# First attention computed transposed, and a second graph's softmax with one wide exponential

## The chip, the cores and the metric

The kernel runs on one core of one Trainium2 chip. The metric is the device time of one execution in microseconds (us). The engines are TensorE (PE, matmuls and transposes into PSUM), VectorE (DVE), ScalarE (ACT), GpSimd (POOL) and SyncE (SP, which issues the DMAs). Each works through its own queue of instructions in order; they wait for each other by semaphores.

## The reference

64 graphs of 128 nodes with 256 features go through four layers, each with a residual and a layer norm. The change touches the first and the last.

```
# layer 0, one graph
query = x @ Wq.T + bq ; keyt = x @ Wk.T + bk ; value = x @ Wv.T + bv
weight = adj * exp(query @ keyt.T)                  # [q, k], no maximum is taken
weight = weight / sum(weight, axis=k)
x = layernorm(x + weight @ value)
# layer 1: three graph convolutions, adj @ (x @ W) + b   (the kernel's gcn_...)
# layer 2: hypergraph convolution up to 512, layer norm, down to 256   (hyper_..., gram)
# layer 3, 8 heads of 32
scores = (q @ k.T) * scale * (2 * adj)              # [head, q, k]
attn = softmax(scores, axis=k)
x = layernorm(x + (attn @ v) @ Wo.T + bo)
```

## The kernel before

Four graphs make a group (`GB = 4`), so there are 16 groups (`NG`). Work on a group has three stages: A is layers 0 and 1, B is layer 2, C is layer 3. In one iteration the kernel does stage A of group t, stage B of group t-1 and stage C of group t-2, interleaved. The order on each engine is written out by hand as a table of step names: `PROLOGUE` (up to t = 2), `SCHEDULE` (12 iterations, t = 3 to 14, the loop is unrolled) and `EPILOGUE`. `run` walks the table; each name is a function for that engine, and the semaphore waits stand in the functions. So the table decides what is queued behind a wait. Weights are split into two fp32r parts (`high_...` by ACT, `rest_...` by DVE) in the prologue, and products are taken as high*high + rest*high + high*rest.

First attention in stage A. `att_t` and `att_t_rest` form t = att^T x, where att is the product of the two weight matrices made once in `set_att`. `att_scores` forms the scores of the four graphs with queries on the partitions. ACT adds a per-row offset in the exponential (`att_exp`, line 867), DVE multiplies by `adjA` (line 1120), PE transposes the four tiles (`att_turn`, line 579), ACT copies them back to SBUF (line 871), and only then `att_out` can multiply them with the values. The column of ones in `v0` makes the row sum, and DVE divides and adds the residual (lines 1125 and 1129). Two adjacency tiles are loaded per group in stage A: `adjA` for the mask and `adjTA`, the transposed one, for the graph convolutions and for `incidence`. The next `adjTA` is loaded only when the last convolution of the group is done.

Last attention in stage C. `mha_scores0` and `mha_scores1` on PE give the scores of graphs 0, 1 and of 2, 3. DVE multiplies each graph's 1024 columns by the mask (line 1245, the DVE step has the same name) and takes the maximum of each of 8 heads (`mha_max`, line 1250). For graphs 0, 1 and 2 ACT then runs 8 exponentials of 128 columns, each with its own bias and its accumulated sum (line 948). For graphs in `WHOLE`, before only graph 3, DVE subtracts the maximum over all 1024 columns (`mha_shift3`, line 1254), ACT runs one exponential of 1024 columns (line 953), and DVE sums (`mha_sum3`, line 1259). DVE takes the reciprocal (`mha_div`), POOL multiplies (line 1377), PE transposes (`mha_turn`, line 788).

Other waits that matter here. `gram` on PE waits for all four residuals of the first attention (`res0_ready`). `hyper_x` of stage B on PE waits until all four masked scores of stage C have left PSUM. `hyper_up01_rest` on PE waits for both halves of `gx_rest`, which DVE makes in `hyper_rest0` and `hyper_rest1` (line 1062). `gcn_1` waits for `gm_ready` from DVE's `gram_scale`. `keep_busy` is four dummy matmuls with `fill`, put where PE would otherwise wait.

## Time and profile before

| | us |
|---|---|
| median of 3 runs | 1061.04 (1059.98 to 1061.5) |
| profiled execution | 1061.14 |
| its span, first to last instruction | 1059.4 |
| PE busy | 1026.7 (97%) |
| DVE busy | 839.8 (79%) |
| ACT busy | 654.5 (62%) |
| POOL busy | 485.2 (46%) |

The busy time of an engine is the union of its instructions' times. A matmul's recorded time is longer than the step from one matmul to the next, because matmuls overlap; so steps between starts are the better measure on PE. In the 12 iterations of the loop the same pattern repeats every 61.4 us.

### The profile page before, as it was taken

To read this page: it belongs to the slowest core of one execution; us is meant where nothing else is said; L and a number is where in the kernel's file an instruction comes from. 1 tells how busy PE (TensorE), PEld (TensorE's weight loads), DVE (VectorE), ACT (ScalarE), POOL (GpSimd) and SP (SyncE) were. 2 spreads that over 40 slices of the span, in tenths; PEclk is the share of its full clock that TensorE was granted. 3 is DMA by queue.
4 is the path that set the end of the run, shared out by engine and by line. 5 is a ranking of instruction groups with operands and counts; after the bars stand their busy time and mean duration, and the time that the engine had idled before them with its cause. 6 is when DMAs were issued, how large, how long until landed. Compare 5 with 4: busy or idle time off the path is not lost.

```text
span 1059.4 us, 21720 instructions
## 1 busy us (share of the span) xinstructions
PE 1026.7 (97%) x8376; PEld 913.4 (86%) x8376; DVE 839.8 (79%) x2247; ACT 654.5 (62%) x1755; POOL 485.2 (46%) x298
## 2 busy tenths in 40 slices
PE   8899999999999999999999999999999999998876
PEld 7688898898989889898988889898988989897764
DVE  4666878878797888879788887978888797978566
ACT  3444855839475683948568394856839485673724
POOL 2315363745435364543536464353546445351613
PEclk9999999999999999999999999999999999999998
DMA  6110101011110101111010111101011110000001
GB/s 228 50 61 9 62 2 61 21 41 51 33 59 21 51 21 41 51 41 50 22 50 22 40 51 41 51 21 50 31 32 51 41 51 21 32 2 11 21 1 40
DMA packets 17383, 43.35 MB, mean 41 GB/s; under 512 B 2048, under 2 KB 2048, under 8 KB 17152
## 3 DMA queue, kind: packets, MB, share of 16 engines
q1 hardware_dynamic: 17280, 41.97, 11.8%
q8 instruction: 66, 1.08, 0.4%
q14 instruction: 37, 0.30, 0.1%
HBM read 33.57 MB, written 8.39 MB: 40 GB/s over the span
## 4 chain that ended last, share of the span: by engine, by line
PE 92%; ACT 3%; DVE 3%; issue 1%; POOL 0%; DMA 0%; POOLq 0%; SPq 0%; DVEq 0%
PE ps L476 83%; PE ps L788 5%; PE ps L729 1%; ACT pr L948 1%; PE ps L579 1%; PE ps L715 1%; DVE pr L1245 1%; PE ps L659 1%; DMA pr<-in_weights 0%; DVE mx L1250 0%; DVE st L1067 0%; DVE aT_rest L1147 0%; ACT aT_high L885 0%; POOL rstd L1331 0%; ACT up_high L925 0%
## 5 line engine op out<-in xcount | busy, mean ns | idle before, releaser
L948 ACT ACTIVATE pr<-pr,mx 128x128 f32<-128x128 f32 x384 | 149.4, 407 | 9.6 <-DVE mx L1250 9.6
L1377 POOL TENSOR_TENSOR pr<-pr,den 128x1024 f32<-128x1024 f32 x64 | 122.1, 1916 | 56.6 <-DVE den L1265 56.6
L1331 POOL TENSOR_TENSOR rstd<-var,neg_half 128x4 f32<-128x4 f32 (+1 forms) x84 | 73.5, 876 | 143.9 <-DVE var L1078 143.9
L1083 DVE TENSOR_SCALAR x<-x,mv,rstd 128x256 f32<-128x256 f32 x256 | 90.6, 417 | 38.8 <-POOL rstd L1331 38.0
L1356 POOL TENSOR_TENSOR x<-x,rows 128x1024 f32<-128x1024 f32 x16 | 38.1, 2381 | 178.6 <-PE ps L476 178.6
L1067 DVE BATCH_NORM_STATS2 st<-x 128x6 f32<-128x256 f32 x256 | 91.6, 415 | 0.7
L1361 POOL TENSOR_TENSOR up_rest<-upT,up_high 128x1024 fp32r<-128x1024 f32 x32 | 81.9, 2561 | 0.0
L1245 DVE TENSOR_TENSOR pr<-ps,adjB 128x1024 f32<-128x1024 f32 x64 | 75.2, 1218 | 7.3 <-PE ps L476 7.3
L948 ACT ACTIVATION_READ_ACCUMULATOR pr<-pr,mx 128x1 f32 x384 | 79.1, 206 | 0.0
L902 ACT COPY s_s<-ps 128x512 f32<-128x512 f32 x32 | 18.8, 587 | 95.2 <-PE ps L476 95.2
L1250 DVE TENSOR_REDUCE mx<-pr 128x8 f32<-128x1024 f32 x64 | 76.4, 1201 | 0.0
L942 ACT ACTIVATE qkT<-ps,biases 128x512 f32<-128x512 f32 x64 | 42.2, 688 | 55.1 <-PE ps L476 54.9
L476 PE MATMUL ps<-W_high,aT_high 128*128 128x256 f32 x256 | 69.9, 298 | 1.9 <-ACT aT_high L885 1.9
L788 PE MATMUL ps<-ident,pr 128*128 128x128 f32 x512 | 67.6, 275 | 3.8 <-POOL pr L1377 1.9
L1366 POOL TENSOR_TENSOR hv<-hv,neg_half 128x2 f32<-128x2 f32 x32 | 22.4, 701 | 103.6 <-DVE hv L1211 103.6
L476 PE MATMUL ps<-W_rest,aT_high 128*128 128x256 f32 x256 | 65.6, 281 | 0.0
L788 PEld LDWEIGHTS ps<-ident,pr 128*128 128x128 f32 x512 | 57.5, 142 | 8.7 <-issue 5.7
L476 PE MATMUL ps<-WdownT_high,up_high 128*128 128x258 f32 x256 | 64.3, 283 | 0.0
L476 PE MATMUL ps<-WdownT_rest,up_high 128*128 128x258 f32 x256 | 63.9, 282 | 0.0
L1269 DVE COPY pr<-ps 128x512 f32<-128x512 f32 x64 | 43.5, 679 | 17.3 <-PE ps L788 17.0
L1350 POOL TENSOR_TENSOR x<-x,rows 128x1024 f32<-128x1024 f32 x16 | 38.6, 2413 | 38.7 <-PE ps L476 38.7
L1147 DVE TENSOR_TENSOR aT_rest<-ps,aT_high 128x512 fp32r<-128x512 f32 x64 | 41.7, 676 | 17.7 <-ACT ps L898 10.9
(199 smaller groups left out, 3310.7 us busy)
## 6 DMA issues: line engine op xcount, KB each, us to landing
xT<-in_xT SPq DMA_DIRECT2D x16, 512.0 KB, 3.7
x<-in_x SPq DMA_DIRECT2D x16, 512.0 KB, 3.3
out_x<-x SPq DMA_DIRECT2D x32, 256.0 KB, 2.1
adjA<-in_adj SPq DMA_DIRECT2D x16, 256.0 KB, 2.7
adjTA<-in_adjT SPq DMA_DIRECT2D x16, 256.0 KB, 2.7
adjB<-in_adj SPq DMA_DIRECT2D x16, 256.0 KB, 2.9
pr<-in_weights SPq DMA_DIRECT2D x2, 512.0 KB, 6.0
qkT<-in_weights SPq DMA_DIRECT2D x1, 1024.0 KB, 12.1
```

What stands on the lines that cost most here:

```text
L476: return pe.matmul(out, lhsT, rhs, start=(k == 0), stop=(k == n - 1))
L788: last = pe.transpose(ps4[:, turn_bank(b) + k // 4, k % 4], pr[:, b, k, :], ident[:])
L942: act.activation(qkT[:, m, :], ps[:, 4 + m, :], ACT.Identity, bias=b_qk[:, m, :], scale=ATT if m < C else 1.0).then_inc(qk_ready, 1)
L948: act.activation(pr[:, b, k, :], pr[:, b, k, :], ACT.Exp, bias=mx[:, b, k:k + 1], accum_out=den[:, b, 0, k:k + 1]).then_inc(exp_ready, 1)
L1067: dve.bn_stats(st[i][:, b, :], t[:, b, :]).then_inc(norm_step[i], 1)
L1083: dve.tensor_scalar(t[:, b, :], t[:, b, :], mv[i][:, b, 0:1], rstd[i][:, b:b + 1], ALU.subtract, ALU.mult).then_inc(ready, 1)
L1245: dve.tensor_tensor(pr[:, b].rearrange("p (j i) n -> p j i n", i=C), ps4[:, 4:8, 2 * bb:2 * bb + 2, :], mask, ALU.mult).then_inc(masked_re ...
L1250: dve.tensor_reduce(mx[:, b, :], pr[:, b], AX.X, ALU.max, negate=True).then_inc(mx_ready, 1)
L1269: dve.tensor_copy(pr[:, b, 4:8, :], ps4[:, turn_bank(b) + 1]).then_inc(prT_dve, 1)
L1331: pool.tensor_tensor(rstd[i][:, bs], var[i][:, bs], neg_half[:, bs], ALU.pow).then_inc(rstd_ready[i], len(pairs))
L1361: pool.tensor_tensor(up_rest[:, fs, :], upT[:, fs, :], up_high[:, fs, :], ALU.subtract).then_inc(up_rest_ready, 1)
L1377: pool.tensor_tensor(pr[:, b], pr[:, b], den[:, b, 1, :].unsqueeze(2).broadcast_to([P, HEADS, P]), ALU.mult).then_inc(pr_ready, 1)
```

## The change

Scores of the first attention are formed transposed, with keys on the partitions. att is now built from the two weight matrices in the other order, and the vectors that carried the biases change places with it (`t0` and the extra column of `Wv0T`). The masked exponential is then already the operand that `att_out` needs: `att_turn` is gone from PE and ACT, and so are the tile `adjA` and its DMA. The mask is now the transposed adjacency, which has two tiles (`adjT[0]`, `adjT[1]`), loaded two groups ahead. `e0` and `p0T` are separate tiles. `WHOLE` becomes (1, 3). `set_att` is split into `set_att` and `set_vec`. All three order tables are new.

```
-WHOLE = (3,)
+WHOLE = (1, 3)
-        adjA = sb("adjA", [P, GB, P]); adjTA = sb("adjTA", [P, GB, P])
+        adjT = [sb(f"adjT{i}", [P, GB, P]) for i in range(2)]
-        e0 = p0 = sb("e0_p0", [P, GB, P])
-        p0T = sb("p0T", [P, N4]); rs0 = sb("rs0", [P, GB]); x0 = sb("x0", [P, GB, D])
+        e0 = sb("e0", [P, GB, P]); p0T = sb("p0T", [P, GB, P]); rs0 = sb("rs0", [P, GB]); x0 = sb("x0", [P, GB, D])
         def att_bank(b):
-            return (b + 2) % 4
+            return (2, 3, 1, 0)[b]
-            def next_adjTA(g):
-                if not final(g):
+            def later_adjT(g):
+                if g + 2 < NG:
                     sp.wait_ge(gcn_done, 2 * g + 2)
                     sp.wait_ge(inc_ready, g + 1)
-                    sp.dma_start(adjTA[:], A["adjT"][g + 1]).then_inc(adjTA_in, 16)
+                    sp.dma_start(adjT[g % 2][:], A["adjT"][g + 2]).then_inc(adjT_in[g % 2], 16)
...
-                        mm(ps[:, m, 0:D], wq0[:, o, m * P:(m + 1) * P], wk0[:, o, :], o, C)
+                        last = mm(ps[:, m, 0:D], wk0[:, o, m * P:(m + 1) * P], wq0[:, o, :], o, C)
+                    last.then_inc(att_mm, 1)
...
-            def att_turn(g):
-                if first(g):
-                    pe.wait_ge(ident_ready, 2)
+            def att_out(g):
                 for b in range(GB):
-                    pe.wait_ge(p0_ready, GB * g + b + 1)
-                    last = pe.transpose(ps4[:, 1, b], p0[:, b, :], ident[:])
-                last.then_inc(p0T_done, 1)
-
-            def att_out(g):
-                pe.wait_ge(p0T_ready, g + 1)
-                for b in range(GB):
+                    pe.wait_ge(p0T_ready, GB * g + b + 1)
...
-            def att_turn(g):
-                act.wait_ge(p0T_done, g + 1)
-                act.copy(p0T[:], ps[:, 1, :]).then_inc(p0T_ready, 1)
...
-                        dve.wait_ge(adjA_in, 16 * g + 16)
-                    dve.tensor_tensor(p0[:, b, :], e0[:, b, :], adjA[:, b, :], ALU.mult).then_inc(p0_ready, 1)
+                        dve.wait_ge(adjT_in[g % 2], 16 * (g // 2) + 16)
+                    dve.tensor_tensor(p0T[:, b, :], e0[:, b, :], adjT[g % 2][:, b, :], ALU.mult).then_inc(p0T_ready, 1)
 SCHEDULE, DVE:
-        ("C", "mha_max0"), ("A", "att_exp"), ("C", "mha_scores1"), ("C", "mha_max1"), ("C", "mha_div0"),
+        ("C", "mha_max0"), ("C", "mha_max1"), ("C", "mha_scores1"), ("C", "mha_max2"), ("C", "mha_shift1"),
```

The order that the tables give shows best in three places. The first is DVE in one iteration of the loop, from `incidence` and the masking of the last attention's scores (`pr<-ps,adjB`, two graphs a row) to `degrees`. `mx` are the maxima, `e_p` or `p0T` the masked exponentials of the first attention, `rs` and `x` its `att_out`, `fT_rest` are `hyper_rest0` and `hyper_rest1`. Before:

```order
411 L1177 TENSOR_TENSOR bhT<-hT,cnt 128x4x128
412 L1245 TENSOR_TENSOR pr<-ps,adjB 128x1024 x2
413 L1250 TENSOR_REDUCE mx<-pr 128x8
414 L1120 TENSOR_TENSOR e_p<-e_p,adjA 128x128 x4
415 L1245 TENSOR_TENSOR pr<-ps,adjB 128x1024 x2
416 L1250 TENSOR_REDUCE mx<-pr 128x8
417 L1265 RECIPROCAL den<-den 128x8
418 L1250 TENSOR_REDUCE mx<-pr 128x8
419 L1125 RECIPROCAL rs<-ps 128x1
```

And now:

```order
417 L1074 TENSOR_SCALAR x<-x,mv,rstd 128x256 x4
418 L1236 TENSOR_TENSOR pr<-ps,adjB 128x1024 x2
419 L1241 TENSOR_REDUCE mx<-pr 128x8 x2
420 L1236 TENSOR_TENSOR pr<-ps,adjB 128x1024 x2
421 L1241 TENSOR_REDUCE mx<-pr 128x8
422 L1245 TENSOR_TENSOR pr<-pr,mx 128x1024
423 L1111 TENSOR_TENSOR p0T<-e,adjT 128x128 x4
424 L1256 RECIPROCAL den<-den 128x8
425 L1053 TENSOR_TENSOR fT_rest<-ps,fT_high 128x512
426 L1116 RECIPROCAL rs<-ps 128x1
```

The mask of the first attention moved behind the second masking and behind the new subtraction (row 422).

The second place is DVE right behind that, up to the layer norm's statistics. Before:

```order
423 L1062 TENSOR_TENSOR fT_rest<-ps,fT_high 128x512
424 L1125 RECIPROCAL rs<-ps 128x1
425 L1129 SCALAR_TENSOR_TENSOR x<-ps,rs,x 128x256
426 L1125 RECIPROCAL rs<-ps 128x1
427 L1129 SCALAR_TENSOR_TENSOR x<-ps,rs,x 128x256
428 L1265 RECIPROCAL den<-den 128x8
429 L1062 TENSOR_TENSOR fT_rest<-ps,fT_high 128x512
430 L1067 BN_STATS st<-x 128x6 x4
```

And now:

```order
431 L1120 SCALAR_TENSOR_TENSOR x<-ps,rs,x 128x256
432 L1116 RECIPROCAL rs<-ps 128x1
433 L1120 SCALAR_TENSOR_TENSOR x<-ps,rs,x 128x256
434 L1250 TENSOR_REDUCE den<-pr 128x8
435 L1053 TENSOR_TENSOR fT_rest<-ps,fT_high 128x512
436 L1256 RECIPROCAL den<-den 128x8
437 L1058 BN_STATS st<-x 128x6 x4
```

A sum over 1024 columns (row 434) now stands in front of the second `fT_rest`.

The third place is ACT at the start of the kernel. `..._high` are the weight splits (`att_high` is the one that `att_t` needs), `xT_high` the split of the input. Before:

```order
1 L978 ACT_TABLE_LOAD
2 L978 CAST WoT_high<-upT 128x512
3 L978 CAST Wv3T_high<-upT 128x512
4 L978 CAST W_high<-pr 128x512
5 L978 CAST att_high<-upT 128x512
6 L978 CAST Wv0T_high<-pr 128x516
7 L906 CAST xT_high<-xT 128x1024
```

And now:

```order
1 L893 ACT_TABLE_LOAD
2 L893 CAST xT_high<-xT 128x1024
3 L965 CAST att_high<-upT 128x512
4 L965 CAST Wv0T_high<-pr 128x516
5 L965 CAST W_high<-upT 128x512
```

The splits of the input and of att now stand ahead of all others.

## Rows read from the trace of the kernel before

**Rows 1.** The page's first part: busy time of each engine.
```profile
PE 1026.7 (97%) x8376; PEld 913.4 (86%) x8376; DVE 839.8 (79%) x2247; ACT 654.5 (62%) x1755; POOL 485.2 (46%) x298
```
**Rows 2.** Busy time by stage: us, each engine's busy (instructions), clock, DMA share, GB/s.
```profile
0.00:25.00 25.00, 21.77 (x79) 18.06 (x80) 10.11 (x43) 8.71 (x13) 5.54 (x9) 1.00 0.64 242
320.00:950.00 630.00, 629.45 (x5326) 567.16 (x5324) 523.26 (x1389) 414.05 (x1107) 312.00 (x185) 1.00 0.11 37
```
**Rows 3.** The same view, one iteration cut at two places on PE.
```profile
481.07:496.56 15.49, 15.49 (x161) 14.20 (x161) 14.58 (x31) 12.46 (x55) 4.43 (x3) 1.00 0.19 52
496.56:542.50 45.94, 45.90 (x362) 41.14 (x361) 36.63 (x109) 27.97 (x55) 25.87 (x16) 1.00 0.11 36
```
**Rows 4.** Timeline of PE there: start, us, what, count.
```profile
481.07 1.17 PE L476 MATMUL ps<-qkT 32*128 32x128 f32 x32
...
489.66 0.60 PE L579 MATMUL ps<-ident,e_p 128*128 128x128 f32 x4
490.10 1.95 PE L476 MATMUL ps<-gmT,x 128*128 128x128 f32 x16
...
495.64 1.16 PE L476 MATMUL ps<-bhT,hT 128*128 128x129 f32 x8
496.56 1.18 PE L476 MATMUL ps<-fT_rest,WupT_high 128*128 128x512 f32 x4
```
**Rows 5.** Waits in two iterations: total us, times, longest.
```profile
PEld ps L476 <- DVE x L1129: 0.9, 2, 0.4
...
PEld ps L788 <- issue: 0.5, 2, 0.2
```
**Rows 6.** Timeline of DVE in the same iteration.
```profile
482.99 2.35 DVE L1245 TENSOR_TENSOR pr<-ps,adjB 128x1024 f32<-128x1024 f32 x2
485.25 1.21 DVE L1250 TENSOR_REDUCE mx<-pr 128x8 f32<-128x1024 f32 x1
486.38 0.89 DVE L1120 TENSOR_TENSOR e_p<-e_p,adjA 128x128 f32<-128x128 f32 x4
487.18 2.35 DVE L1245 TENSOR_TENSOR pr<-ps,adjB 128x1024 f32<-128x1024 f32 x2
...
492.52 0.17 DVE L1125 RECIPROCAL rs<-ps 128x1 f32<-128x1 f32 x1 [0.67 <-PE ps L476]
...
493.72 0.68 DVE L1062 TENSOR_TENSOR fT_rest<-ps,fT_high 128x512 fp32r<-128x512 f32 x1
494.31 0.16 DVE L1125 RECIPROCAL rs<-ps 128x1 f32<-128x1 f32 x1
...
501.24 1.19 DVE L1254 TENSOR_TENSOR pr<-pr,mx 128x1024 f32<-128x1024 f32 x1
```
**Rows 7.** The page: exponentials of the last attention, one head each.
```profile
L948 ACT ACTIVATE pr<-pr,mx 128x128 f32<-128x128 f32 x384 | 149.4, 407 | 9.6 <-DVE mx L1250 9.6
```
**Rows 8.** Timeline of ACT in the same iteration: one exponential over 1024 columns.
```profile
505.28 1.07 ACT L953 ACTIVATE pr<-pr 128x1024 f32<-128x1024 f32 x1
```
**Rows 9.** Timeline of ACT at the start of the kernel.
```profile
14.66 0.62 ACT L978 CAST WoT_high<-upT 128x512 fp32r<-128x512 f32 x1 [12.64 <-DMA upT<-in_weights]
```
**Rows 10.** Timeline of PE at the start of the kernel.
```profile
13.01 3.76 PE L476 MATMUL ps<-fill 128*128 128x512 f32 x8
...
20.80 0.58 PE L476 MATMUL ps<-xT_high,att_high 128*128 128x512 f32 x1
...
30.02 1.00 PE L579 MATMUL ps<-ident,e_p 128*128 128x128 f32 x4
31.69 2.01 PE L476 MATMUL ps<-v,p0T 128*128 128x257 f32 x8 [0.68 <-ACT p0T L871]
```
**Rows 11.** Timeline of DVE at the start of the kernel.
```profile
28.44 1.23 DVE L1056 TENSOR_TENSOR WdownT_rest<-pr,WdownT_high 128x1032 fp32r<-128x1032 f32 x1
```
**Rows 12.** Timeline of PE near the end of the kernel.
```profile
974.34 1.09 PE L476 MATMUL ps<-fill 128*128 128x512 f32 x4
...
992.21 1.06 PE L788 MATMUL ps<-ident,pr 128*128 128x128 f32 x8 [0.95 <-ACT upT L928]
```

More of the change, by code:

```diff
@@ new lines @@
+    "DVE": [("set_rep", 0), ("set_att", 0), ("rest_att", 0), ("set_vec", 0), ("rest_Wv0T", 0), ("set_reps", 0),
+        ("incidence", 0), ("rest_Wv3T", 0), ("rest_W2", 0), ("rest_WupT", 0), ("set_down", 0), ("att_exp", 0),
[22 rows of a table added]
+        ("high_WupT", 0), ("high_Wv3T", 0), ("att_v1", 0), ("att_off", 0), ("att_t", 0), ("att_exp", 0),
[18 rows of a table added]
+    "SP": [("att_scores", 0), ("att_out", 0), ("gcn_3a1", 0), ("att_scores", 1), ("att_out", 1), ("att_scores", 2),
+        ("gcn_3a1", 1), ("mha_scores1", 0), ("att_out", 2), ("x3_norm1", 0), ("x3_norm0", 0)],
@@ L645, in gcn_3a @@
                 for b in (2 * pair, 2 * pair + 1):
-                    last = mm(ps2[:, 2 + pair, b % 2], adjTA[:, b, :], s3[:, b, :])
+                    last = mm(ps2[:, 2 + pair, b % 2], adjT[g % 2][:, b, :], s3[:, b, :])
                 last.then_inc(gcn_done, 1)
```

97 lines of the change are left out of this document (46 added, 51 removed), and 302 rows, old and new, of tables (EPILOGUE, PROLOGUE, SCHEDULE).

## The prediction

> **What bounds the kernel now.** I read the page's busy times first: PE is busy 97% of the span, DVE 79%, ACT 62% [rows 1]. Then the busy time by stage: from 320 to 950 us PE is busy 629.45 of 630 us at the full clock, while in the first 25 us it is busy 21.77, part of that with dummy matmuls [rows 2]. So the loop is bound by PE, and a change is worth there what it does to PE's row of instructions; the ends of the kernel are bound by chains between engines. Third the timelines of one iteration [rows 4, 6]. One iteration lasts 61.43 us and I cut it where the last attention's scores start on PE (`mha_scores0`, 481.07) and where `hyper_up01_rest` starts (496.56): 15.49 and 45.94 us [rows 3]. In the first piece DVE is itself busy 14.58 of 15.49 us, in the second 36.63 of 45.94 [rows 3]. The reader is to see that the first piece is the one place of the loop where a second engine has hardly any room, and that the change puts DVE work just there. Fourth the waits: in the loop PE hardly waits, twice a short time per iteration [rows 5].
>
> **What it takes away on PE.** `att_turn` is 4 transposes; from their start to the next instruction 0.44 us pass (489.66 to 490.10) [rows 4]. That is 0.44 us per iteration at full value as long as PE bounds. The ACT copy behind it, the load of `adjA` and one SP queue entry go too; neither ACT (12.46 of 15.49 us in the piece) nor DMA (share 0.19) sets anything in the loop [rows 3], so I count them at nothing, and the cover that hides them is PE's own work. The second `adjT` tile frees the mask from waiting for a load; no row shows a wait for `adjTA` or `adjA` in the loop, so it is nothing too, below and above.
>
> **The wide exponential for graph 1.** ACT loses 8 exponentials of 128 columns, each 0.407 us long by the page [rows 7], and gets one of 1.07 us [rows 8]: 8 x 0.407 - 1.07, some 2 us of ACT per iteration, off the path in the loop. DVE gets a subtraction of 1.19 us and a sum over 1024 columns, which is the same kind of instruction with the same shape as the maximum, 1.21 us; the step from the maximum to the next instruction is 1.13 (485.25 to 486.38), so I count 1.1 for each of the two [rows 6]. So DVE carries 2.2 us more, and both stand in the tight piece.
>
> A rule of the Trainium skill speaks against this half: VectorE: DVE Perf Modes, section Rules for kernel authors, calls `tensor_reduce` the slowest DVE operation and advises to restructure where it is on a hot path. The rows show it no slower than the subtraction of the same width, 1.21 us for the maximum against 1.19 [rows 6]; by the rule the sum would cost more than the term below takes, by the rows it costs the same. It is the place, not the kind, that costs here.
>
> **The tight piece step by step.** DVE cannot start masking before the scores end on PE, 1.17 us into the piece [rows 4], about 0.05 later. Before, it came late (482.99), because `x1_norm` waited for POOL and `incidence` stood behind it [rows 6]; in the new order `incidence` stands ahead of `x1_norm`, fills that wait, and DVE is there in time. Then it has, up to the end of `hyper_rest1`, without a gap: two maskings of two graphs at 2.26 (482.99 to 485.25), three maxima at 1.13, the subtraction 1.1, the four masks of the first attention 0.80 (486.38 to 487.18), a reciprocal 0.1, `hyper_rest0` 0.59 (493.72 to 494.31), four rows of `att_out` at 1.20 a pair (492.52 to 493.72), the sum 1.1, and `hyper_rest1` to its end 0.68 [rows 6]. That is 4.52 + 3.39 + 1.1 + 0.80 + 0.1 + 0.59 + 2.40 + 1.1 + 0.68 = 14.68. With 1.17 in front and 0.05 at either end the piece lasts 15.95 us. PE alone needs 15.49 less 0.44 for the transposes and less about 0.15 for its wait before `gram`, which DVE's line 1129 ends (0.4 on the weight load, most of it under the matmul in front) [rows 5]: 14.9. So I expect PE to wait about 1.05 us there, 0.2 of it before `att_out` (the masks now stand behind the subtraction and come about when PE arrives) and 0.85 before `hyper_up01_rest`, because the sum stands in front of `hyper_rest1`. Behind that wait on PE are `hyper_up2`, `hyper_up3` and all the rest, in order, and everyone waits for PE. The piece grows by 15.95 - 15.49 = 0.46 us although PE has less to do.
>
> In the other piece `mha_turn1` no longer follows `mha_turn0` at once, which takes away a stall of 0.2 [rows 5]; DVE's `gram_scale` comes about when `gcn_1` wants it, which I put at 0.1 of wait. Net -0.1. Per iteration +0.36, for 12 iterations +4.3 us. Bounds: if no new wait showed, -0.44 - 0.15 - 0.2 = -0.8 an iteration, -9.6 in all; if both new DVE instructions (2.3 us) fell wholly on PE, less 0.8, +1.5 an iteration, +18. I take the value of the count, nearer to the lower row since PE has 14.9 us of cover.
>
> **The start.** Before, ACT's first instruction is a weight split that waits 12.64 us for its DMA, and the splits for `att_t` stand behind it; PE runs dummies for 3.76 us from 13.01 on and then `set_down`, before `att_t` starts at 20.80 [rows 9, 10]. Now `xT_high` and `att_high` come first, the dummies run while the first DMA is awaited, and `set_down` comes behind `att_v1`, when its weights have landed. So about 3.6 us of dummies leave the path (3.76 less the overlap with the next matmul). The first `att_turn` and its copy leave it too: 30.02 to 31.69, 1.67 us [rows 10]. Against that DVE's `rest_WdownT` (1.23 us, 1.15 as a step) now stands between the two halves of `att_out` [rows 11]. -3.6 - 1.67 + 1.15 = -4.1. Bounds: 0, if the DMA of `WupT`, whose split now stands ahead of `att_t` on ACT, holds it as long; -7, if all that stands between the first matmuls and 20.80 but `set_down` were gained as well.
>
> **The end.** The dummies before `mha_scores1` of group 14 go (974.34, 1.09 us recorded, some 0.9 as a step), and `mha_turn1` waits 0.95 us less for ACT, whose exponentials are shorter [rows 12]; in the last group the third POOL product comes some 0.6 earlier by the 2 us less on ACT against the DVE work put in. -2.5, with bounds -5 and +2, since DVE's two wide instructions lie on the chain of the last group, and a dummy in another place can let PE's clock fall, which the trace shows only at the very end.
>
> **The sum.** The profiled execution took 1061.14 us (span 1059.4), the median is 1061.04. 1061.04 + 4.3 - 4.1 - 2.5 = 1058.7 us. A measurement of this kernel tells about 0.2% (2.1 us) from no change.
>
> **Rivals.** (1) PE stays the only bound in the loop: DVE's row is shorter than I add it up, or PE's is longer, so that the new waits vanish. -0.8 x 12 - 4.1 - 2.5 gives 1044.8. For it: PE is busy 99.9% now [rows 2], and the order of before had only some 0.15 us of waits in the same piece. Against it: the step lengths are from rows of the same instructions, and they add up to more than PE's. This is also what Perfetto Trace Analysis of the Trainium skill, section Identifying the Most-Contended Engine, would make of it: relieve the engine with the highest occupancy first; by it the transposes count in full.
> (2) DVE's delay runs on. `max3`, `degrees`, `x0_norm` and `shift3` follow the sum, and `gram_scale` stands behind all of them; PE's `gcn_1` waits for it. I have PE arrive 0.1 before it. From that point each further 0.1 us on DVE costs 0.1 on PE; with 0.3 us on the first piece and 0.3 at `gcn_1` it is 0.6 more an iteration, +7.2: 1066. For it: DVE and POOL work side by side there, and DVE has no gap from the scores on. Against it: DVE is busy only 36.63 of the 45.94 us [rows 3].
> (3) The start and end gain nothing, since later waits take it back, and only the loop counts: 1065.3. Against it: the first 25 us are not full of needed work: 21.77 us busy with the dummies counted in [rows 2, 10].
>
> **Chances.** My count 0.47, its own range 1054.5 to 1062; rival 1 0.26; rival 2 0.17; rival 3 0.10. Faster by over 0.2% (below 1058.9): all of rival 1 and a bit over half of the count, 0.52. Within 0.2% (to 1063.2): 0.20, from the count. Slower: rivals 2 and 3, 0.28 with a rest of the count. The range 1046 to 1067 leaves 0.1 on each side: below it half of rival 1, above it the tail of rival 2.
>
> **What would show it.** In the changed kernel's trace: one iteration of 61.8 us; from the first `qkT` matmul to the first `fT_rest` matmul 15.9 us; PE waiting for `fT_rest` of DVE some 0.8 us in each iteration, and for `p0T` 0.2. If the iteration is 60.6 us with no such wait, rival 1 holds; if PE waits for DVE's `gm` at `gcn_1` as well, rival 2. `att_out` of the first group should start near 27.5 us instead of 31.69. The forecast is wrong if the iteration is under 61.4 us, or if the first group's `att_out` starts later than 30 us.

## The result, and the profile after

The changed kernel takes 1063.6 us (median of 10 runs, 1061.88 to 1065.28) against 1059.63 us (10 runs, 1059.07 to 1061.57) for the kernel before, measured beside each other: ratio 1.0033, 95% interval 1.0023 to 1.0042. It is slower by 4 us; I had forecast 1058.7, faster. Its profiled execution took 1061.88 us (span 1060.1), the one before 1061.14 (span 1059.4), so the two traces differ by 0.7 us only. The other 3.3 us lie between the profiled executions and the medians: the one of before stands 1.5 us above its median, the one of after 1.7 us below.

For the changed kernel the granted clock of TensorE goes along with this in the main. Its ten runs show a mean granted clock of 0.994 at spans of 1060.1 to 1060.7, of 0.992 at 1061.6 to 1061.9 and in one run at 1063.5, and of 0.990 at 1062.8 to 1062.9. The trace has three stretches at half clock (1.2 of 2.4 GHz): 3.4 us at 29.5, 6.8 us at 1029.6 and the last 3.2 us. For the kernel before the mean clock explains nothing: its runs beside the experiments lie at 1058.7 to 1059.8 us or at 1060.9 to 1062.1 us with the same mean clock of 0.995. What parts those two groups stays open.

The page's first part, after (against [rows 1]):

```profile
PE 1017.9 (96%) x8300; PEld 900.0 (85%) x8300; DVE 897.8 (85%) x2278; ACT 608.1 (57%) x1499; POOL 492.1 (46%) x298
PE 73%; DVE 20%; issue 3%; ACT 2%; DMA 1%; POOL 1%; SPq 0%; POOLq 0%; DVEq 0%
```

PE has 8.8 us less to do, DVE 58 us more, ACT 46 us less. Of DVE's 58 us some 23 are no work: an addition of 512 columns (`sqs<-sqs,upT`) takes 2.46 us in the mean instead of 0.68 in 13 groups, where it now meets POOL (last section). PE does not wait for it. The second line is the chain that ended last: a fifth of it is DVE now. Busy time of one iteration, cut at the same two places as [rows 3] (us, then PE, PE's weight loads, DVE, ACT, POOL, clock, DMA share, GB/s):

```profile
478.30:494.45 16.15, 15.48 (x157) 13.87 (x156) 15.11 (x28) 11.78 (x49) 4.24 (x2) 1.00 0.14 43
494.45:540.46 46.01, 46.01 (x356) 41.05 (x356) 39.98 (x115) 25.48 (x45) 26.70 (x16) 1.00 0.09 32
```

This iteration is the longest of the twelve, 62.17 us. The others have 62.03 to 62.07 (the last 61.26, where before it was 60.76), and their first piece is 16.03 or 16.04. The next one:

```profile
540.46:556.50 16.04, 15.36 (x158) 13.87 (x157) 15.01 (x28) 11.90 (x49) 4.25 (x2) 1.00 0.15 47
556.50:602.51 46.01, 46.01 (x357) 41.04 (x357) 39.98 (x115) 25.50 (x45) 26.70 (x16) 1.00 0.09 31
```

PE in that stretch (answers to [rows 4]):

```profile
478.30 1.17 PE L465 MATMUL ps<-qkT 32*128 32x128 f32 x32
...
486.89 1.95 PE L465 MATMUL ps<-gmT,x 128*128 128x128 f32 x16
488.94 2.01 PE L465 MATMUL ps<-v,p0T 128*128 128x257 f32 x8
...
492.73 1.16 PE L465 MATMUL ps<-bhT,hT 128*128 128x129 f32 x8
494.45 1.21 PE L465 MATMUL ps<-fT_rest,WupT_high 128*128 128x512 f32 x4 [0.56 <-DVE fT_rest L1053]
```

PE's waits over six iterations (total, times, longest; answers to [rows 5]):

```profile
PE ps L465 <- DVE fT_rest L1053: 3.4, 6, 0.6
```

DVE (answers to [rows 6]):

```profile
479.54 2.36 DVE L1236 TENSOR_TENSOR pr<-ps,adjB 128x1024 f32<-128x1024 f32 x2 [0.89 <-PE ps L465]
481.81 2.33 DVE L1241 TENSOR_REDUCE mx<-pr 128x8 f32<-128x1024 f32 x2
484.07 2.35 DVE L1236 TENSOR_TENSOR pr<-ps,adjB 128x1024 f32<-128x1024 f32 x2
486.35 1.21 DVE L1241 TENSOR_REDUCE mx<-pr 128x8 f32<-128x1024 f32 x1
487.47 1.22 DVE L1245 TENSOR_TENSOR pr<-pr,mx 128x1024 f32<-128x1024 f32 x1
488.60 0.89 DVE L1111 TENSOR_TENSOR p0T<-e,adjT 128x128 f32<-128x128 f32 x4
489.41 0.20 DVE L1256 RECIPROCAL den<-den 128x8 f32<-128x8 f32 x1
489.61 0.69 DVE L1053 TENSOR_TENSOR fT_rest<-ps,fT_high 128x512 fp32r<-128x512 f32 x1
...
492.59 1.21 DVE L1250 TENSOR_REDUCE den<-pr 128x8 f32<-128x1024 f32 x1
493.72 0.68 DVE L1053 TENSOR_TENSOR fT_rest<-ps,fT_high 128x512 fp32r<-128x512 f32 x1
```

The reader is to see that DVE has no gap from 479.54 to the end of `hyper_rest1` at 494.4, and that PE's step from the start of the `bhT,hT` matmuls to the first `fT_rest` one is 1.72 us where it was 0.92 [rows 4] (1.69 in the other iterations). A smaller wait, 0.28 us, stands ahead of the `v,p0T` matmuls: the step from `gmT,x` to them is 2.06, and 1.78 in runs where they need not wait (mask_first, no_shift).

The start, PE and then ACT (answers to [rows 10] and [rows 9]):

```profile
10.75 0.50 PE L465 MATMUL ps<-xT_high,att_high 128*128 128x512 f32 x1 [1.20 <-DVE att_rest L1047]
...
21.38 2.05 PE L465 MATMUL ps<-xT,tT 128*128 128x128 f32 x16 [0.95 <-ACT tT L840]
...
24.21 2.01 PE L465 MATMUL ps<-v,p0T 128*128 128x257 f32 x8
```

```profile
17.61 1.04 ACT L965 CAST WupT_high<-qkT 128x1024 fp32r<-128x1024 f32 x1 [1.21 <-DMA qkT<-in_weights]
18.57 0.61 ACT L965 CAST Wv3T_high<-upT 128x512 fp32r<-128x512 f32 x1
...
20.08 1.25 ACT L840 ACTIVATE tT<-ps,t 128x512 f32<-128x512 f32 x2
```

A ledger from the start of `mha_scores0` of each group on PE, after less before: group 0 -6.7 us, group 1 -5.9, group 13 (twelve iterations of the loop later) +1.5, the end of the span +0.7. The loop begins with group 1. So in these two profiled executions the start gave 5.9 us, the loop cost 7.4 (62.04 us an iteration against 61.42), and the end gave 0.8.

Only the loop's part is the same from run to run. Twelve of the runs below have the changed kernel's tables ahead of the loop. In their traces `mha_scores0` of group 1 starts at 168.2 to 170.6 us (168.06 in the changed kernel's, 173.93 before), and from group 13 to the end they take 148.0 to 149.4 us (148.2, and 149.0 before). The profiled execution of after is thus a lucky one at its start. Against the one trace of before the start gave 3.3 to 5.9 us, and the end something between a gain of 1.0 and a loss of 0.5.

### The profile page after: what moved, and what is told of

Same layout as the page of the kernel before. It is cut to its first block, busy times and chain, and to the rows that moved or that the text cites. A ratio compares the mean times of both kernels' runs of the same rounds, so it can differ in the third digit from the quotient of the medians.

```text
span 1060.1 us, 21374 instructions
## 1 busy us (share of the span) xinstructions
PE 1017.9 (96%) x8300; PEld 900.0 (85%) x8300; DVE 897.8 (85%) x2278; ACT 608.1 (57%) x1499; POOL 492.1 (46%) x298
## 3 DMA queue, kind: packets, MB, share of 16 engines
q8 instruction: 65, 1.06, 0.4%
## 4 chain that ended last, share of the span: by engine, by line
PE 73%; DVE 20%; issue 3%; ACT 2%; DMA 1%; POOL 1%; SPq 0%; POOLq 0%; DVEq 0%
PE ps L465 65%; DVE pr L1236 5%; PE ps L775 5%; DVE mx L1241 5%; DVE x L1120 3%; DVE pr L1245 2%; DVE den L1250 1%; PE ps L716 1%; DMA qkT<-in_weights 1%; DVE fT_rest L1053 1%; PE ps L702 1%; PE ps L646 1%; DVE rs L1116 1%; DVE p0T L1111 0%; DVE x L1074 0%
## 5 line engine op out<-in xcount | busy, mean ns | idle before, releaser
L1322 POOL TENSOR_TENSOR rstd<-var,neg_half 128x4 f32<-128x4 f32 (+1 forms) x84 | 80.4, 957 | 121.4 <-DVE var L1069 119.7
L935 ACT ACTIVATE pr<-pr,mx 128x128 f32<-128x128 f32 x256 | 99.6, 402 | 9.9 <-DVE mx L1241 9.9
L1352 POOL TENSOR_TENSOR up_rest<-upT,up_high 128x1024 fp32r<-128x1024 f32 x32 | 76.6, 2394 | 3.0 <-ACT upT L915 3.0
L912 ACT ACTIVATE up_high<-ps,biases 128x512 fp32r<-128x512 f32 x64 | 44.1, 688 | 30.9 <-PE ps L465 30.8
L1341 POOL TENSOR_TENSOR x<-x,rows 128x1024 f32<-128x1024 f32 x16 | 38.3, 2391 | 42.6 <-PE ps L465 42.6
L925 ACT CAST fT_high<-ps 128x512 fp32r<-128x512 f32 x32 | 17.2, 590 | 66.8 <-PE ps L716 66.8
L465 PE MATMUL ps<-W_high,aT_rest 128*128 128x256 f32 x256 | 53.5, 292 | 1.2 <-DVE aT_rest L1138 1.2
L465 PE MATMUL ps<-fT_high,WupT_high 128*128 128x512 f32 x128 | 53.6, 418 | 0.7 <-ACT fT_high L908 0.7
```

The source lines that it names most:

```text
L465: return pe.matmul(out, lhsT, rhs, start=(k == 0), stop=(k == n - 1))
L912: act.activation(up_high[:, f, :], ps[:, 4 + f, :], ACT.Relu, bias=b_up[:, f, :]).then_inc(up_high_ready, 1)
L935: act.activation(pr[:, b, k, :], pr[:, b, k, :], ACT.Exp, bias=mx[:, b, k:k + 1], accum_out=den[:, b, 0, k:k + 1]).then_inc(exp_ready, 1)
L1322: pool.tensor_tensor(rstd[i][:, bs], var[i][:, bs], neg_half[:, bs], ALU.pow).then_inc(rstd_ready[i], len(pairs))
L1352: pool.tensor_tensor(up_rest[:, fs, :], upT[:, fs, :], up_high[:, fs, :], ALU.subtract).then_inc(up_rest_ready, 1)
```

## Experiments

Every run was timed in five rounds beside the kernel before; ratios are to that. "Iteration" is the distance of two `mha_scores0` on PE in the middle of the loop, from the run's trace. Apart from one or two iterations in a run it repeats within some 0.05 us, so differences in the loop are read from it; a median carries the spread of both ends as well. A, B, C in the tables are the three groups at work in an iteration.

### sum_late: the sum behind hyper_rest1

```diff
 SCHEDULE, DVE
-("C", "mha_sum1"), ("B", "hyper_rest1"), ("C", "mha_div1"),
+("B", "hyper_rest1"), ("C", "mha_sum1"), ("C", "mha_div1"),
```

> The changed kernel with mha_sum1 behind hyper_rest1 in the loop's table. Theory A (the loop is lost to the place of the sum): in the changed kernel PE waits 0.73 us before the first fT_rest matmul of every iteration, with hyper_rest1 standing behind the 1.1 us sum. With the sum behind it the iteration falls from 62.06 us to about 61.35, 12 iterations give -8.5 us, so about 1055 us against 1063.6. Theory B (DVE is late as a whole, rival 2 of the prediction): everything behind the sum stands where it did, PE arrives at gcn_1 0.7 us earlier and waits there for gm instead; the iteration stays at 61.9 to 62.1 and the time at 1062 to 1064.

1064.39 us, ratio 1.0037 (1.0025 to 1.005), iteration 62.20. The wait before `fT_rest` is gone and this one has come, at `gcn_1` (timeline of PE):

```profile
503.34 0.49 PE L465 MATMUL ps<-aT_high,W_high 128*128 128x512 f32 x1 [0.46 <-DVE gm L1186]
```

Theory B held, with an iteration 0.1 us above its range: moving the sum behind `hyper_rest1` wins nothing and costs 0.16 us.

### mask_first: the first attention's mask ahead of the subtraction as well

```diff
 SCHEDULE, DVE, on top of sum_late
-("C", "mha_shift1"), ("A", "att_exp"),
+("A", "att_exp"), ("C", "mha_shift1"),
```

> As sum_late, and in the loop the mask of the first attention (att_exp) also ahead of mha_shift1. Theory A: the other new wait, 0.28 us of PE around att_out, goes as well: iteration 61.05 to 61.1 us, some 3 us less than sum_late in all, about 1052 us. Theory B: no more than sum_late. A third way: the subtraction, now 0.8 us later, makes the wide exponential late on ACT, then the sum and the division on DVE, and mha_turn1 on PE waits: iteration above sum_late's.

1064.96 us, ratio 1.0044 (1.0031 to 1.0057), iteration 62.19. The wait ahead of `v,p0T` is gone, PE waits some 0.2 us for `att_out`'s `x` at `gram` instead (from `v,p0T` to `bhT,hT` it takes 3.94 us, 3.70 in sum_late), and for `gm` as before. It is no more than sum_late, as theory B said.

### narrow and turn_back: without the wide exponential, in the new order

```diff
 SCHEDULE (narrow: PROLOGUE and EPILOGUE too)
-DVE: ("C", "mha_shift1"), ("C", "mha_sum1")
-ACT: ("C", "mha_exp1")
+ACT: ("C", "mha_exp1a"), ("C", "mha_exp1b")
 turn_back alone, PE:
-("C", "mha_turn0"), ("A", "gcn_ax"), ("C", "mha_turn1")
+("A", "gcn_ax"), ("C", "mha_turn0"), ("C", "mha_turn1")
```

> The changed kernel with only the last graph's softmax wide: no subtraction and no sum for graph 1 on DVE, 8 exponentials of one head each on ACT again. This leaves the attention half of the change and the new tables. Theory A (the wide exponential's 2.3 us on DVE are the whole loss of the loop): both new waits go, PE needs 62.06 - 0.73 - 0.28 = 61.05 us an iteration, total about 1051 to 1053 us. Rival (the attention half with its later mask and new order costs too, or ACT with 2 us more becomes late for mha_turn1 by up to 0.5): iteration 61.4 or more, 1056 us or more.

1072.5 us, ratio 1.0118 (1.0102 to 1.0133), iteration 62.42. Theory A missed. The figures lie in the rival's open range, but by another wait than it named, 1 us at `mha_turn0` and not up to 0.5 at `mha_turn1`. PE's waits over six iterations:

```profile
PE ps L776 <- ACT upT L916: 6.3, 6, 1.1
PE ps L466 <- DVE x L1121: 1.1, 6, 0.2
```

`mha_turn0` waits for a part of PSUM that ACT's `up_out` rows free, and these stand behind 2 us more of exponentials. In the traces it is 10.2 us longer than the changed kernel: 1.7 us ahead of the loop, 4.6 in it and 4.0 behind it.

> As narrow, but narrow in the loop's groups only, and mha_turn0 on PE behind gcn_ax again, as in the kernel before. In narrow PE waited 1.2 us an iteration at mha_turn0 for the up_out rows of ACT, behind 3.2 us of narrow exponentials. Theory (the wide exponential is there to let mha_turn0 stand ahead of gcn_ax): with 1.9 us of gcn_ax as cover the wait goes, iteration 61.0 to 61.3 us, 1051 to 1054 us. Rival (ACT's row stays late and holds gcn_1 through axT instead): 61.8 or more.

1061.5 us, ratio 1.0013 (1.0005 to 1.0022), iteration 61.97. The theory missed and the rival's figure held. The wait moved to `mha_turn1`: the step from `mha_turn0` to it is 1.72 us where 8 transposes take 0.87. So in the new order the loop takes as long with narrow exponentials as with the wide one (62.04), in one case for ACT and in the other for DVE.

### old_loop: the attention half alone, in the old order

```diff
-SCHEDULE = the changed kernel's
+SCHEDULE = the kernel before's, without its three ("A", "att_turn") entries
+wide exponential for graph 1 only in groups 0 and 13 to 15
```

> The changed kernel's attention, start and end (with the wide exponential for graph 1 in the first and the last three groups), but in the loop the order of the kernel before with only its att_turn entries taken out, and eight narrow exponentials for graph 1. This is the attention half alone in the loop. Theory (the transposes leave PE, and no row of another engine gets longer): the kernel before's iteration of 61.42 us less 0.44 for the transposes and up to 0.2 of waits: 60.8 to 61.0 us, 12 times 1.1 us below the changed kernel: 1049 to 1052 us. Rival (the mask on DVE or the ACT row, gapless from 486.7 to 503 us in the kernel before, holds PE): 61.3 or more, 1055 or more.

1051.49 us, ratio 0.9917 (0.9904 to 0.9931). One iteration:

```profile
474.31:535.28 60.97, 60.97 (x517) 54.95 (x516) 51.08 (x138) 40.00 (x108) 30.30 (x18) 1.00 0.11 36
```

60.98 us, 0.44 below the kernel before: as much as the four transposes took. PE has no idle time in it. The changed kernel is 1.06 us an iteration and 12 us in all above this. That is the price of the wide exponential together with the order that was made for it; turn_back shows that taking only the exponential back wins nothing.

### wide_before: the other half alone, in the old order

```diff
 all three tables of the kernel before; in SCHEDULE:
 DVE: ("C", "mha_max1"), +("C", "mha_shift1"), ... ("B", "hyper_rest1"), +("C", "mha_sum1"), ("C", "mha_div1")
 ACT: -("C", "mha_exp1b"), -("C", "mha_exp1a"), +("C", "mha_exp1")
```

> The kernel before with the wide exponential for graph 1 as well and nothing else: the subtraction behind mha_max1, the sum behind hyper_rest1 and ahead of mha_div1, one exponential over 1024 columns in place of eight. The transposes of the first attention stay. Theory B: DVE's row from the masking of the scores to gram_scale has one gap of 0.67 us before att_out in the kernel before; the two instructions lengthen it by 2.27 - 0.67 = 1.6 us; PE's slack at gcn_1 is some 0.3 to 0.6: iteration 62.4 to 62.7 us, total 1072 to 1076. Rival (ACT's row, gapless too from 486.7 to 503 us in the kernel before, was the tighter one and is 2 us shorter): no loss, iteration 61.3 to 61.5, total about 1060.

1089.81 us, ratio 1.0281 (1.0264 to 1.0297), iteration 63.00: +1.58, the whole 1.6 by which the row grew; the slack at `gcn_1` that I took off is not there. This is the wide exponential with nothing else changed in the loop. The total came out above its range: besides the loop's 19 us the profiled execution is 1.5 us longer ahead of the loop and 4.5 behind it, where the same edit stands too, and the median is 3.5 us above the profiled execution. Theory B had counted none of this. PE waits for DVE's `x` before `gcn_ax` and before `gram`.

### two_sums and no_shift: DVE 1.1 us longer, and 1.1 us shorter

```diff
 mha_sum, two_sums (groups 1 to 12, graph 1)
+dve.tensor_reduce(den[:, b, 1, :], pr[:, b], AX.X, ALU.add)
 dve.tensor_reduce(den[:, b, 0, :], pr[:, b], AX.X, ALU.add).then_inc(sum_ready, 1)
 mha_shift, no_shift (groups 1 to 12, graph 1)
-dve.tensor_tensor(pr[:, b], pr[:, b], mx[:, b, :]..., ALU.add).then_inc(shift_ready, 1)
+dve.tensor_copy(mx[:, b, 0:1], mx[:, b, 0:1]).then_inc(shift_ready, 1)
```

> The changed kernel with the sum over graph 1's exponentials made twice in the loop's groups, 1.13 us more in the same place of DVE. Theory R: DVE's row bounds the iteration with nothing to spare, so the whole 1.1 us appear: iteration 63.1 to 63.2 us, total about 1076 to 1077 us. Rival (PE's 0.73 us wait before fT_rest only moves): 62.1 to 62.6 us, 1064 to 1071 us.

1076.7 us, ratio 1.0152 (1.0139 to 1.0166), iteration 63.17: the whole 1.13 us, as theory R said.

> The changed kernel, with the subtraction of the maximum left out for graph 1 of the loop's groups (the exponential takes the scores as they are). Everything stands where it stood; DVE has 1.14 us less between the scores and gram_scale. Theory R (the gapless row of DVE from mha_scores0 to the copies of mha_turn sets the iteration, whatever its order): the iteration falls by 0.9 to 1.1, to where PE bounds it, 61.0 to 61.1 us; total about 1051 to 1052 us. Rival (the waits of the changed kernel come from somewhere else too, ACT or POOL): 61.4 or more.

1063.4 us, ratio 1.0027 (1.0017 to 1.0038), iteration 62.03: nothing. Theory R is wrong for the subtraction. DVE's timeline shows why:

```profile
487.83 0.14 DVE L1246 COPY mx<-mx 128x1 f32<-128x1 f32 x1
487.89 0.89 DVE L1111 TENSOR_TENSOR p0T<-e,adjT 128x128 f32<-128x128 f32 x4
489.00 0.20 DVE L1259 RECIPROCAL den<-den 128x8 f32<-128x8 f32 x1 [0.22 <-ACT pr L935]
489.96 0.69 DVE L1053 TENSOR_TENSOR fT_rest<-ps,fT_high 128x512 fp32r<-128x512 f32 x1 [0.76 <-ACT fT_high L908]
```

`hyper_rest0` now waits 0.76 us for ACT's cast of `hyper_x`, which waits for PE, and `att_out` stands behind `hyper_rest0` on DVE. It starts 11.3 us into this iteration with the subtraction (489.61 - 478.30) and without it (489.96 - 478.65), and 11.2 in the others of both runs. The gapless row in the changed kernel was two chains that end together there. The idle time shows how much room the subtraction had: 0.22 + 0.76 us for an instruction that was shortened by 1.08. It fitted almost exactly.

### gm_first and norm_first: what else stands in the row

```diff
 SCHEDULE, DVE, gm_first on top of sum_late
-("C", "mha_shift3"), ("A", "gram_scale"),
+("A", "gram_scale"), ("C", "mha_shift3"),
 norm_first on top of gm_first (the same steps, moved)
+("A", "x0_stats"), ("C", "mha_sum1"), ("C", "mha_div1"), ("A", "degrees"), ("A", "x0_norm"),
+("A", "gram_scale"), ("C", "mha_max3"), ("C", "mha_shift3"),
 SCHEDULE, POOL, norm_first
-("C", "mha_div1"), ("A", "x0_stats"),
+("A", "x0_stats"), ("C", "mha_div1"),
```

> sum_late, and gram_scale ahead of mha_shift3 in the loop's table of DVE. In sum_late the wait before fT_rest is gone, but PE waits 0.62 us at gcn_1 for gm and 0.3 at gcn_ax for x0_norm; the iteration was 62.20 us. Theory B (one gapless row of DVE work from mha_scores0 to gram_scale bounds this stretch; what stands in it that PE does not want yet is what costs): the subtraction's 1.14 us leave the row, the wait at gcn_1 goes wholly and the one at gcn_ax stays: iteration 61.55 to 61.65 us, about 1057.5 us in all. Rival (the subtraction is wanted there): mha_exp3, the sum, the division on POOL and mha_turn3 come late, and PE waits before mha_turn3 instead: iteration 62 us or more.

1065.21 us, ratio 1.0051 (1.0038 to 1.0064), iteration 62.17: the rival. The wait at `gcn_1` is gone and PE waits about as long for POOL's product before `mha_turn3`:

```profile
PE ps L775 <- POOL pr L1368: 2.1, 6, 0.4
```

> gm_first, and the layer norm of the first attention ahead of the sum of graph 1: hyper_rest1, x0_means1, x0_means0, x0_stats, mha_sum1, mha_div1, degrees, x0_norm, gram_scale, mha_max3, mha_shift3; on POOL x0_stats ahead of mha_div1. Theory B: the 0.3 us at gcn_ax go too, and the wide exponential costs PE nothing: iteration 61.1 to 61.3 us, below the 61.42 of the kernel before, about 1052 to 1054 us. Rival: mha_div1 on POOL, now behind x0_stats, ends later than mha_turn1 wants it, or mha_shift3 makes mha_turn3 late: 61.6 or more.

1098.29 us, ratio 1.0369 (1.0354 to 1.0383), iteration 64.0 to 65.4, far off both. DVE first, then POOL:

```profile
513.15 2.75 DVE L1074 TENSOR_SCALAR x<-x,mv,rstd 128x256 f32<-128x256 f32 x4
...
518.33 2.25 DVE L1245 TENSOR_TENSOR pr<-pr,mx 128x1024 f32<-128x1024 f32 x1
```

```profile
512.88 1.90 POOL L1368 TENSOR_TENSOR pr<-pr,den 128x1024 f32<-128x1024 f32 x1 [0.35 <-DVE den L1256]
517.11 2.38 POOL L1341 TENSOR_TENSOR x<-x,rows 128x1024 f32<-128x1024 f32 x1 [2.34 <-PE ps L465]
519.46 3.37 POOL L1352 TENSOR_TENSOR up_rest<-upT,up_high 128x1024 fp32r<-128x1024 f32 x1
```

The four norms take 2.75 us instead of 1.35 and the subtraction 2.25 instead of 1.22; they end 1.1 us after POOL's instructions do (at 514.78 and 519.49). POOL's next one, begun while DVE's subtraction ran, takes 3.37 instead of 2.38. The order that I gave them made DVE and POOL collide three times an iteration; the third is `sqs<-upT`, 2.08 us in the median where its shortest is 0.68.

That is not all of it. The iterations come in two lengths, and TensorE's clock parts them (the columns of [rows 3]; the last but two is the clock):

```profile
364.98:429.04 64.06, 61.40 (x513) 54.76 (x513) 58.06 (x141) 37.52 (x94) 31.46 (x18) 1.00 0.10 34
429.04:494.38 65.34, 62.89 (x513) 55.95 (x513) 57.29 (x141) 37.64 (x94) 31.44 (x18) 0.97 0.10 33
```

Eight of the twelve iterations hold a stretch of 3.4 us at half clock, and each of these is 1.3 us longer. Ahead of it PE had waited 1.9 us for DVE's copies (`pr L1260`) in each iteration, also in the four that kept the full clock. So at full clock the new order costs 1.9 us an iteration against gm_first (64.05 against 62.17), some 22 us, and the lower clock adds some 10. The collisions are the cause that the rows show for the 1.9; no run has this order without them.

### no_shift_late and all_three: both chains at once

```diff
 no_shift_late = no_shift + sum_late
 all_three: SCHEDULE, DVE, on top of that
-("C", "mha_div0"), ("B", "hyper_rest0"), ("A", "att_out"),
+("C", "mha_div0"), ("A", "att_out"), ("B", "hyper_rest0"),
```

> no_shift (the subtraction for graph 1 left out in the loop) together with sum_late (the sum behind hyper_rest1). Each alone gave nothing: 62.03 and 62.20 us an iteration. Theory T (two chains of the same length end at hyper_rest1: DVE's own row of maskings, maxima, subtraction and sum; and PE's hyper_x, the cast on ACT, hyper_rest0, att_out and the sum. Sum_late frees the second and moves the first, as a row, to gcn_1; no_shift frees only the first): together they take the sum out of the one and 1.14 us out of the other: iteration 61.0 to 61.2 us, total 1051 to 1053 us. Rival (what is lost is bound elsewhere, by POOL's products or ACT's row): 61.7 or more, 1060 or more.

1065.6 us, ratio 1.0052 (1.0037 to 1.0066), iteration 62.20: theory T fell and the rival's figure held. `hyper_rest0` starts 11.2 us into the iteration, as in sum_late, and from there to `gram_scale` nothing is shorter.

> no_shift_late, and att_out ahead of hyper_rest0 on DVE, as in the kernel before. Theory U: DVE's row starts with the first att_out instead of hyper_rest0, 10.9 instead of 11.2 us into the iteration, and has the same length: gm comes 0.3 us earlier, iteration 61.8 to 62.0 us, total 1060 to 1063 us. Rival (hyper_rest0's place is the whole loss): 61.1 to 61.3 us, 1052 to 1055 us.

1063.34 us, ratio 1.0026 (1.0017 to 1.0036), iteration 62.00, as theory U said, at the upper edge of its ranges: the place of `hyper_rest0` is worth 0.2 us.

### no_sum and short_sum: is it the sum?

Both leave work out, so the kernel's output is wrong: no_sum takes one column of each head for the sum, short_sum two of 128.

```diff
 mha_sum, groups 1 to 12, graph 1
-dve.tensor_reduce(den[:, b, 0, :], pr[:, b], AX.X, ALU.add).then_inc(sum_ready, 1)
+dve.tensor_copy(den[:, b, 0, :], pr[:, b, :, 0]).then_inc(sum_ready, 1)             # no_sum
+dve.tensor_reduce(den[:, b, 0, :], pr[:, b, :, 0:2], AX.X, ALU.add).then_inc(...)   # short_sum
```

> The changed kernel with the sum over graph 1's exponentials left out in the loop's groups (a copy of 8 columns stands in its place); the subtraction stays. Theory U (from hyper_rest0, which waits for ACT's cast of hyper_x 11.2 us into the iteration, DVE has one gapless row to gram_scale, and only what stands in that row costs: the sum, not the subtraction ahead of it): the wait of 0.73 us before fT_rest goes and none comes at gcn_1, iteration 61.0 to 61.2 us, total 1050.5 to 1053 us. Rival (as with no_shift another chain is just as long): 61.7 or more, 1060 or more.

1066.42 us, ratio 1.0055 (1.0042 to 1.0069), iteration 62.31, which looks like a refutation. DVE's row and POOL's:

```profile
495.58 1.35 DVE L1251 COPY den<-pr 128x8 f32<-128x8 f32 x1
```

```profile
494.52 2.37 POOL L1350 TENSOR_TENSOR x<-x,rows 128x1024 f32<-128x1024 f32 x1
```

A copy of 8 columns took 1.35 us. POOL's addition ran until 496.89, the copy ended at 496.93. The experiment had put a wait of 1.2 us where it took a sum of 1.13 us away.

> The changed kernel with the sum for graph 1 in the loop's groups taken over 2 columns a head instead of 128: the same kind of instruction in the same place, about 0.16 us instead of 1.21. Theory U (what stands in DVE's row behind hyper_rest0 costs, and a reduction doesn't wait for POOL as the copy of no_sum did): the wait of 0.73 us before fT_rest goes, iteration 61.0 to 61.2 us, total 1050.5 to 1053 us. Rival P (any short instruction there waits for POOL's addition): as no_sum, 62.3 us and 1066. Rival C (another chain just as long, as with no_shift): 61.7 to 62.0, 1060 to 1063.

1055.02 us, ratio 0.9948 (0.993 to 0.9965), iteration 61.20, and PE has no wait in the loop that the waits view lists. In DVE's timeline, in the same place and beside the same addition on POOL:

```profile
490.02 0.16 DVE L1251 TENSOR_REDUCE den<-pr 128x8 f32<-128x16 f32 x1
490.10 0.68 DVE L1053 TENSOR_TENSOR fT_rest<-ps,fT_high 128x512 fp32r<-128x512 f32 x1
```

Theory U held, rivals P and C did not. 61.20 us is still 0.22 above old_loop; the wait of 0.28 us ahead of `v,p0T` is left in it. The total came 2 us above its range, with six runs between 1052.17 and 1058.67. The loop gave the 10 us forecast in the trace, while the start was 1.6 us longer and the end 1.2 longer than in the changed kernel's profiled execution, both within what other runs with the same tables show there.

### start, both, attention_start, attention_end: the ends

```diff
 start: PROLOGUE
 ACT: x_high, high_att, high_Wv0T, att_t, att_v0, att_v1, att_off, att_exp, high_W1, high_W2, high_W3, high_WupT, ...
 PE:  ..., att_v1, att_scores, set_wo, att_out, set_down, gram, ...
 DVE: the rests of W2, WupT, Wv3T and WdownT and set_down behind gcn_ax of group 0
 both = norm_first + start + four dummy matmuls behind set_vec;  attention_start = old_loop + start
 attention_end = attention_start, and in EPILOGUE, PE, last group:
+("keep_busy11", 1), ("keep_busy12", 1), ("mha_scores1", 1), ... +("keep_busy13", 1), ("mha_ctx0", 1)
```

> The changed kernel with another start: on ACT att_t ahead of every weight split that waits for a DMA after 13.8 us, on PE set_down behind att_out, the splits of W2, WupT, Wv3T and WdownT into later gaps of DVE. In the changed kernel the first scores wait for tT, which stands on ACT behind the split of WupT, landed at 17.6 us. Theory A (ACT's order holds the start): the first att_out starts at about 20.5 us instead of 24.2 and the gain of 3 to 4 us lasts to the loop: about 1060.5 us. Theory B (DVE's work on weights and norms sets the start and only moves): att_out early, but gcn_1 or the first hyper_up late again, gain under 1 us in all, about 1063 us.

1060.62 us, ratio 1.0004 (0.9993 to 1.0015), 3 us below the changed kernel by the medians and 0.4 by the profiled executions. The first `att_out` starts at 22.13, not 20.5: the granted clock was half from 10.0 to 16.8 us, just under the matmuls of `att_t` and `att_v`. At the first `fT_rest` on PE 1.3 us of the gain are left in the profile (65.12 against 66.44).

> norm_first with the start of the run start, and four dummy matmuls more on PE between set_vec and att_t, where PE had no work for 1.2 us. The run start had the first att_out at 22.13 us instead of 24.22, though the granted clock was half from 10.1 to 16.9 us there. Theory: the two changes add up, and with the clock held the first att_out starts at about 19 to 20 us: norm_first less 1.3 to 4 us, about 1049 to 1052 us. Rival: the start's gain is taken back by the weights' splits, or the clock falls all the same: no more than 1 us below norm_first.

1093.81 us, ratio 1.0327 (1.0313 to 1.0341). It carries norm_first's collisions, so it says nothing of the loop; less norm_first it is 4.5 us, and the first `att_out` starts at 21.52.

> old_loop with the start of the run start. Nothing couples the two: old_loop's 1051.5 less the 1.3 us that the run start kept at the first loop iteration in its profile (up to 3 us by its median): 1048.5 to 1050.2 us. Rival: the start's gain was only other stretches at half clock: 1051 to 1052 us.

1047.92 us, ratio 0.9888 (0.9874 to 0.9902), 3.6 us below old_loop (3.1 by the two ratios).

> attention_start with dummy matmuls on PE in two waits of the last group: eight ahead of mha_scores1, where PE waited 2.48 us, and four ahead of mha_ctx0, where it waited 1.37. In the last group a stretch of 3.4 us at half clock began some 1.3 to 3 us behind each of these waits. Theory (an idle PE lets the clock fall): one or both stretches go, 1 to 2.5 us less than attention_start. Rival (dummies delay the real matmuls or the stretches come all the same): no change or up to 1 us more.

1047.33 us, ratio 0.9883 (0.987 to 0.9897); iteration 60.97, first `att_out` at 19.63, with the full clock from 5.8 to 36.5 us. The last group, from its `mha_scores0` on, in attention_start and then here:

```profile
1012.30:1045.50 33.20, 23.08 (x228) 18.50 (x228) 24.58 (x44) 12.60 (x42) 8.94 (x6) 0.85 0.09 33
1012.30:1045.50 33.20, 23.78 (x240) 18.27 (x240) 24.46 (x44) 12.68 (x42) 8.93 (x6) 0.97 0.09 33
```

The stretch at half clock from 1015.0 to 1021.8 is gone, that at the very end stays. The theory held for the clock and missed for the time: the group ends at the same place, 33.3 us after its scores in both traces, and the medians differ by 0.6 us, within the spread of four runs each. With attention_start this is the fastest version, 12 us below the kernel before.

## Why the prediction was wrong

**What bounds it: right.** PE bounds the loop and the tight piece is where DVE decides [rows 2, 3]. I read DVE's 14.58 of 15.49 us in it rightly as having no room.

**The transposes: right.** 0.44 us forecast, 0.44 measured by old_loop, whose order in the loop is that of before without them.

**The tight piece: right in kind and nearly in size.** Forecast were 15.95 us with waits of 0.2 and 0.85; measured are 16.04, with 0.28 and 0.78 by PE's steps (2.06 against 1.78, 1.69 against 0.91). DVE's row takes 14.86 us where I added up 14.68. The gain of 0.15 ahead of `gram` did not come: in all_three, which has neither wait, PE takes 15.05 us for the piece and not 14.9. Yet the row that I added up was not the only one (no_shift): the cast of `hyper_x` on ACT ends with it, and the new order puts `hyper_rest0` in front of `att_out`. Of the two instructions that I priced alike at 1.1 us, the subtraction costs nothing (no_shift, 62.03) and the sum nearly all of its length: 0.84 us came back for 1.05 taken out (short_sum, 61.20), 1.13 for 1.13 put in (two_sums, 63.17). So the size came out partly by luck: without the subtraction the piece is the same 16.04 us.

**The other piece: wrong by 0.18.** I forecast -0.1 for it, measured is +0.08 (46.01 against 45.93). The stall between the two turns did go, 0.20 us for the 16 transposes, and `gcn_1` has no wait. But the matmuls of `gcn_ax` take 0.11 us more, and many small steps behind `gcn_1` 0.14 more in sum, against the kernel before. I had put that stretch of the new order at nothing without a reason.

**The loop: the step that failed.** "Per iteration +0.36, for 12 iterations +4.3" was +0.62 and +7.4: 0.54 from the first piece where I had 0.46, and 0.08 from the other where I had -0.1. Rival 2 (DVE's delay runs on to `gram_scale`) is not what the changed kernel's trace shows, but it is what stands right behind: as soon as the wait before `fT_rest` is taken away, it is at `gcn_1` (sum_late), and then at `mha_turn3` (gm_first). I had treated it as a case of its own; it is the same row, which is too long by the sum wherever the wait shows. The 14.9 us of PE's work that I called cover are none for it: the row starts with a cast that waits for PE's own `hyper_x`, 11.2 us into the iteration.

**The start: right in sign, short in size.** -4.1 forecast, -5.9 measured where the loop begins (-3.3 to -5.9 over the runs with these tables, so the sum is closer than its working). The first `att_out` starts at 24.2 us, not 27.5. I let only the dummies leave the path. In fact `att_t` starts 10.05 us earlier on PE (10.75 against 20.80); of that 5.7 us are left at the first scores (21.38 against 27.07), which wait for `tT`. The clock is granted at full from 5.6 us instead of 18.5. That eight dummies without a gap behind them did this, where before four were followed by 1.72 us of waiting, is not shown: in other runs with the same start the clock came to full at 4.5 to 7.7 us, and in eight of the twelve it fell again for 3.4 or 6.8 us from 10 to 12 us on. Both of my bounds had a part of the truth: -7 for what could be gained, and ACT, where `att_t` stands behind the split of `WupT`, for what is not.

**The end: hardly any of it came.** -2.5 forecast, -0.8 in the profiled execution, and -1.0 to +0.5 over the runs with these tables. Where the rest stays was not looked for.

**The run-to-run part: not in the sum.** The account of the whole, in us:

| term | forecast | measured |
|---|---|---|
| loop | +4.3 | +7.4 |
| start | -4.1 | -5.9 |
| end | -2.5 | -0.8 |
| from the profiled executions to the medians | 0 | +3.3 |
| sum | -2.3 | +4.0 |

So the loop missed by 3.1 us and the end by 1.7, which the start made up for by 1.8, and the last term missed by 3.3. I took the three runs of before as typical (median 1061.04, profiled 1061.14), but all ten have their median at 1059.63. The changed kernel's profiled execution is in turn 1.7 us below its median. The traces of the other runs show where such a difference can lie, at both ends of the kernel. Why a run takes the longer way there is open; that attention_end's dummies removed one stretch at half clock and no time speaks against the clock of the last group as the cause.

## What to carry to other kernels

When work is added to an engine inside a tight stretch, find the event that starts its row (here a cast that another engine delivers 11 us in). What stands ahead of it is free as long as it fits in the idle time there (here 0.98 us, found by taking an instruction out), what stands behind it costs nearly in full, and a reordering only moves the wait. An experiment that takes an instruction away must put nothing in its place that waits for something else; read the replacement's own duration before believing the total. Two changes that come in one diff are to be timed apart: here the one was worth -5 us in the loop, and the other with its new order +12. A difference of a few us between two medians is to be traced to a place before it is explained: here the loop repeats within 0.05 us, while start and end differ by 2.6 and 1.5 us between runs with the same tables.
